# Graph attention on one core: the context is divided on VectorE between two transposes, ScalarE copies two squares of groups 3 to 7, and SyncE's loads and stores stand between two groups' transfers

## The reference, cut to what matters

```
q = _heads(x @ Wq + bq); k = _heads(x @ Wk + bk); v = _heads(x @ Wv + bv)
scores = einsum('bhqd,bhkd->bhqk', q, k) / sqrt(64)
probs  = softmax(scores + where(adj, 0.0, -9e15)[:, None], axis=-1)
ctx    = einsum('bhqk,bhkd->bhqd', probs, v)          # heads put side by side again
out    = layernorm(x + ctx @ Wf + bf)
```

## Time and profile before

| | |
|---|---|
| Median of 3 runs | 1295.83 us (1287.64 to 1299.62) |
| The profiled execution's own time | 1290.07 us |
| Its span on the core | 1288.3 us, granted clock 0.974 |
| Busy share PE / DVE / ACT / POOL | 92% / 76% / 63% / 44% |
| Shares of the chain that ended last | PE 55%, SP's queue 17%, DVE 12%, DMA 7%, ACT 4% |
| DMA engines busy, mean | 76.7% for SyncE's queue, 1.9% for ScalarE's |
| Squares moved by DMA | 1528 from SyncE and 8 from ScalarE, 128 KB each, median 2.4 us from issue to landing |

### The profile page before, as it was taken

The page is one execution under the profiler, slowest core; times in us unless marked ns, Lnnn a source line. Parts: engine busy times, 40 slices in busy tenths (PEclk is TensorE's granted clock), DMA queues, the critical chain, the costliest instruction groups (busy, mean ns, idle before and its releaser), DMA issues.

```text
span 1288.3 us, 24781 instructions
## 1 busy us (share of the span) xinstructions
PE 1187.8 (92%) x8790; PEld 891.4 (69%) x8790; DVE 984.5 (76%) x1535; ACT 807.7 (63%) x1628; POOL 560.8 (44%) x943
## 2 busy tenths in 40 slices
PE   6998999899998899988999989998999889999874
PEld 5866777566776677766787667776777667786653
DVE  5788877778677886878868878688876778778782
ACT  5666765657665676666666676666775657656551
POOL 1234643446524454344543544344643436433432
PEclk9999999999998999989999999999999989999998
DMA  5688787977879777888778888789787887878784
GB/s 161 154 202 228 181 206 189 230 195 176 204 189 237 180 185 196 194 214 203 188 195 194 220 203 210 180 207 239 182 201 199 207 204 174 212 172 203 193 201 109
DMA packets 111611, 251.71 MB, mean 195 GB/s; under 512 B 27904, under 2 KB 62336, under 8 KB 111488
## 3 DMA queue, kind: packets, MB, share of 16 engines
q1 hardware_dynamic: 107296, 243.58, 76.7%
q10 hardware_dynamic: 4192, 6.56, 1.9%
HBM read 36.11 MB, written 12.58 MB: 38 GB/s over the span
## 4 chain that ended last, share of the span: by engine, by line
PE 55%; SPq 17%; DVE 12%; DMA 7%; ACT 4%; issue 4%; POOL 1%; ACTq 0%; POOLq 0%; DVEq 0%
PE context_ps L538 19%; SPq L308 16%; PE score_ps L523 13%; PE job_ps L425 7%; DMA prob_t<-prob 6%; PE job_ps L427 6%; PE job_ps L426 6%; DVE prob L735 6%; DVE prob L728 4%; ACT prob L628 3%; PE job_ps L459 2%; DVE res L750 1%; SPq L388 1%; PE job_ps L435 0%; PE score_ps L435 0%
## 5 line engine op out<-in xcount | busy, mean ns | idle before, releaser
L728 DVE CUSTOM_DVE_ANT_0 prob<-score_ps,mask 128x1024 f32<-128x1024 f32 x384 | 454.8, 1222 | 225.1 <-PE score_ps L523 163.5
L628 ACT ACTIVATE prob<-prob,row_min 128x1024 f32<-128x1024 f32 x384 | 440.2, 1148 | 213.3 <-DVE row_min L728 212.5
L735 DVE STREAM_TRANSPOSE prob<-prob 128x1024 f32<-128x1024 f32 x384 | 457.8, 1230 | 38.8 <-ACT prob L628 38.8
L538 PE MATMUL context_ps<-prob_t,v_all 128*64 128x256 f32 x3072 | 373.0, 398 | 61.9 <-DMA prob_t<-prob 61.8
L538 PEld LDWEIGHTS context_ps<-prob_t,v_all 128*64 128x64 f32 x3072 | 239.4, 144 | 166.9 <-issue 82.1
L850 POOL TENSOR_TENSOR context<-context_raw,context 128x256 f32<-128x256 f32 x96 | 70.8, 738 | 337.5 <-ACT context_raw L645 337.1
L523 PE MATMUL score_ps<-k_hi,q_hi 64*128 64x512 f32 x768 | 141.1, 445 | 4.5 <-DVE row_min L728 3.6
L425 PE MATMUL job_ps<-xt_hi,weight_hi 128*128 128x256 f32 (+1 forms) x423 | 142.0, 336 | 0.0
L427 PE MATMUL job_ps<-xt_hi,weight_lo 128*128 128x256 f32 (+1 forms) x423 | 135.6, 320 | 0.0
L426 PE MATMUL job_ps<-xt_lo,weight_hi 128*128 128x256 f32 (+1 forms) x423 | 135.5, 320 | 0.0
L523 PE MATMUL score_ps<-k_lo,q_hi 64*128 64x512 f32 x768 | 120.9, 392 | 0.0
(11 more groups left out here) (78 smaller groups left out, 1659.5 us busy)
## 6 DMA issues: line engine op xcount, KB each, us to landing
prob_t<-prob SPq DMA_DIRECT2D x1528, 128.0 KB, 2.4
res<-in_x_dram SPq DMA_DIRECT2D x32, 384.0 KB, 4.3
out_dram<-res SPq DMA_DIRECT2D x32, 384.0 KB, 2.9
adj_in<-in_adj_dram SPq DMA_DIRECT2D x31, 256.0 KB, 3.0
x_in<-in_x_dram SPq DMA_DIRECT2D x16, 384.0 KB, 3.5
x_in<-in_x_dram ACTq DMA_DIRECT2D x14, 384.0 KB, 4.5
prob_t<-prob ACTq DMA_DIRECT2D x8, 128.0 KB, 4.8
res<-in_x_dram SPq DMA_DIRECT2D x1, 768.0 KB, 6.8
```

What stands on the lines that cost most here:

```text
L538: last = pe.matmul(context_ps[64 * head:64 * head + 64, 0:GQ], v_all[:, kt, col:col + HS], keys, start=(kt == 0), stop=(kt == TT - 1))
L628: nc.scalar.activation(probabilities(t), probabilities(t), ACT.Exp, scale=-1.0, bias=row_min[:, ring:ring + 1], accum_out=row_sum[:, s // ...
L728: nc.vector.tensor_tensor_reduce(probabilities(t), in_quarters(score_ps[:, head, :]), in_quarters(mask[:, s % 2, :]), 1.0, HUGE, ALU.add, ...
L735: nc.vector.transpose(probabilities(t), probabilities(t)).then_inc(squared, 1)
```

## The change

It has three parts.

1. VectorE multiplies the context straight out of PSUM, between the two turns of the slot that has the mix (`divide` moves from the block of GpSimd to that of VectorE). `take_context`, the buffer `context_raw` and the semaphore `context_out` go; the next mix waits for `context_done` instead.
2. For groups 3 to 7, two of the four squares that stay on their partitions (a = 2 and 3) are no longer moved by DMA: ScalarE copies them (`keep_square`) at the end of slots 2g+2 and 2g+3, one in each, so in slots 8 to 17.
3. SyncE's loads and stores move from odd slots, where they stood between the halves of a group's transfers, to even slots, and the load of the second half of x goes from ScalarE's queue to SyncE's, at slots 12 and 14. Two of GpSimd's additions of the output bias to the residual (`RESIDUALS`) move later with their loads.

```diff
+OWN_GROUPS = (3, 4, 5, 6, 7)
+OWN = (2, 3)
-STORES = {1: -2, 9: -1, 13: 0, 21: 1}
-RES_LOADS = {2: 0, 10: 1, 14: 2, 22: 3}
-X_LOADS = {4: (0, 0), 6: (0, 1)}
-RESIDUALS = {2: -1, 6: 0, 13: 1, 17: 2}
+STORES = {2: -2, 10: -1, 16: 0, 20: 1}
+RES_LOADS = {4: 0, 12: 1, 18: 2, 22: 3}
+X_LOADS = {4: (0, 0), 6: (0, 1), 12: (1, 0), 14: (1, 1)}
+RESIDUALS = {2: -1, 6: 0, 14: 1, 20: 2}
...
                 for a in range(4):
-                    move_square(queue, group, a, (a + ahead) % 4)
+                    if ahead or group not in OWN_GROUPS or a not in OWN:
+                        move_square(queue, group, a, (a + ahead) % 4)
...
             def mix(b, group):
-                pe.wait_ge(context_out, at(b, GROUPS, group + 2))
+                pe.wait_ge(context_done, at(b, GROUPS, group + 2))
...
-            def take_context(b, group):
-                act.wait_ge(mixed, at(b, GROUPS, group + 3))
-                act.wait_ge(context_done, at(b, GROUPS, group + 2))
-                nc.scalar.activation(context_raw[:], context_ps[:, 0:GQ], ACT.Copy).then_inc(context_out, 1)
+            def keep_square(b, group, a):
+                act.wait_ge(squared, at(b, UNITS, 4 * group + 4))
+                act.wait_ge(mixed, at(b, GROUPS, group + 1))
+                own = slice(32 * a, 32 * a + 32)
+                nc.scalar.activation(prob_t[own, group % 2, a].rearrange("p q h n -> p (q h n)"),
+                                     prob[own, group % 2, a].rearrange("p q h n -> p (q h n)"),
+                                     ACT.Copy).then_inc(landed[group % 2], 16)
...
-                        if job[0] == "m":
-                            take_context(b, job[1])
-                        elif job[0] != "p" and job not in early:
+                        if job[0] not in "pm" and job not in early:
                             evict(b, job)
-                            if job == ("x", FT - 1, 0, 1):
-                                for i in range(2):
-                                    load_x(nc.scalar, b, 1, i)
                     for group in contexts_split(b.mode, s):
                         if s - 1 not in SPLIT_LATER:
                             context_high(b, group)
+                    if s // 2 - 1 in OWN_GROUPS:
+                        keep_square(b, s // 2 - 1, OWN[s % 2])
...
+            def divide(b, group):
+                dve.wait_ge(mixed, at(b, GROUPS, group + 3))
+                dve.wait_ge(job_out, out_through(b, ("i", group, 0, 0)))
+                nc.vector.tensor_tensor(context[:], context_ps[:, 0:GQ], context[:],
+                                        ALU.mult).then_inc(context_done, 1)
...
                         turn_squares(b, 2 * s)
+                    for job in work:
+                        if job[0] == "m":
+                            divide(b, job[1])
+                    if s < SLOTS:
                         turn_squares(b, 2 * s + 1)
```

More of the change, by code:

```diff
@@ L157, in graph_attention @@
         raw = sb("raw", [P, 2, 512], F32)
-        context_raw = sb("context_raw", [P, GQ], F32)
         context = sb("context", [P, GQ], F32)
@@ L207, in graph_attention @@
         mixed = sem("mixed")
-        context_out = sem("context_out")
         context_done = sem("context_done")
@@ L419, in _ @@
             pe.sem_inc(mixed, 2)
-            pe.sem_inc(context_out, 2)
             pe.sem_inc(projected, 4)
@@ L702, in _ @@
             dve.sem_inc(masked, 2)
+            dve.sem_inc(context_done, 2)
             dve.sem_inc(sum_done, 8)
@@ L818, in _ @@
             pool.sem_inc(context_lo_done, 1)
-            pool.sem_inc(context_done, 2)
             pool.sem_inc(normalised, 4)
@@ L845, in low_part @@
                 nc.gpsimd.tensor_tensor(lo, copy[:, 0:width], hi, ALU.subtract).then_inc(lo_done, 1)
-            def divide(b, group):
-                pool.wait_ge(context_out, at(b, GROUPS, group + 3))
-                pool.wait_ge(job_out, out_through(b, ("i", group, 0, 0)))
-                nc.gpsimd.tensor_tensor(context[:], context_raw[:], context[:], ALU.mult).then_inc(context_done, 1)
             def context_low(b, group):
@@ L862, in body @@
                     for job in work:
-                        if job[0] == "m":
-                            divide(b, job[1])
                         if job[0] in "kqx":
```

## The result

The changed kernel takes 1247.82 us (median of 4 runs, 1245.41 to 1248.31) against 1297.72 us beside it (1287.64 to 1301.90); the ratio is 0.9623 with a 95% interval of 0.9564 to 0.9681, so it is 3.8% faster. The forecast was 1250, in a range of 1236 to 1272. The profiled execution took 1245.41 us with a span of 1243.6, against a predicted 1249. The runs of the kernel before lie 14.3 us apart, those of the changed kernel 2.9.

The account below looks back on a forecast made before the run. Late squares, from SyncE's issue and x loads, bound slots 8 to 17. Windows fall from 455.47 to 413.6 us (gain 42), tail 2, less 3 for the clock: 41 off 1290.07 gives 1249, predicted 1250, range 1236 to 1272.

Parts of the forecast that it names:

- What bounded the kernel: Slots 8 to 17: TensorE waits 61.8 us for late squares, and a stall also costs about 2 us of slower matmuls.
- The sum of the windows: Slot 8's first mask to slot 17's, eight batches: 413.6 us against 455.47, a gain of 42; one window 51.7.
- Transfers no longer end the waits: Groups 3 to 7: 14 transfers land 11 to 12 us after the last turn; waits on them fall under 10 us.
- three signs of being wrong: Wrong if windows stay above 55 us, mixes still last over 5 us, or copies pass 1.3 us.
- The copy: End of odd slots: ScalarE's copy takes 1.05 us (0.9 to 1.2) and sets the next mask after slots 9, 11, 13.
- The division: VectorE, between the turns: 0.43 us (0.38 to 0.55); even slots take 5.42 to 5.5 us, 0.1 to 0.2 over undisturbed.
- The worth of the division: Gains where ScalarE's high part delayed an exponential, 0.6 us in slot 11, and 2 us in the last batch's tail.
- The share of the order: Slot 12's stall is late issue plus 3.4 us of x, slot 16's issue alone; x now moves while no mix waits.
- The clock: Rival, chance 0.12: slot 14's stall, or summed stalls of slots 10 to 16, bring 1.2 GHz; 1261, up to 1270.
- The slow copy: Rival, chance 0.04: each us of copy over 1.05 costs nearly 4 us a batch; at 2.8 us a copy 1303.
- The tail: Last batch: two short chains behind its mixes go, 0.8 us each, a gain of 2 us.
- The step from the profiled execution to the median: Runs' median lies 5.8 us above the profiled execution, but that spread goes with the stalls: 1249 profiled, 1250 predicted.

Follow-up runs that it names:

- copies_even: The changed kernel with both ScalarE copies of a group at the end of even slot 2g+2, none in odd slots; 1237.90 us, ratio 0.9542.
- the longer copy: The changed kernel with ScalarE first copying 384 more elements in odd slots into a buffer that nothing reads; 1265.89 us.
- one_each: The changed kernel with a group's two copies in even slots, one on ScalarE and one on GpSimd, 14 transfers; 1231.61 us, ratio 0.9501.

## Why the prediction was right, step by step

- **What bounded the kernel.** Right: the late squares of groups 3 to 7 and the slow mixes behind them. The sum of the windows, on which the forecast rests, carries all but 0.2 of the 44.7 us of span.
- **Transfers no longer end the waits.** Right in slots 10 to 18, where ScalarE's copy ended 30 of VectorE's waits. A group of 3 to 7 has landed 11.2 to 11.5 us after its last turn, as said (11 to 12). Waits for transfers were said to fall under 10 us; they are 13.3 and 11.3: TensorE's have one of 6.9 before the last mix, VectorE's are for groups that still have 16 transfers. And of the three signs of being wrong one is there by its words, a mix of over 5 us; it is the last of the kernel and outside the windows that the forecast was about.
- **The copy.** 1054 ns against 1.05 predicted. Slots 9, 11 and 13 take 6.57, 6.56 and 6.33 us against 6.35, 6.35 and 6.1. Two small things were missed: the copy starts 0.03 us after its predecessor's end, not 0.1 before it, and mask and mix start 0.14 after its end, not 0.05. Slot 15 takes 5.60 as predicted, though the sum given for it (5.43 and 0.3) makes 5.73.
- **The division.** 423 ns against 0.43. Even slots take 5.3 us, not 5.42 to 5.5: the predicted lag of 0.1 to 0.2 us lies within the time until the next scores are ready. This error (0.8 us a window) and the copy's (0.7) have opposite signs, so the sum of a window came out at 51.57 against 51.7 by luck as well as by working.
- **The worth of the division.** Here the text was too modest. It named 0.6 us in slot 11 and 2 us at the tail. Alone it is worth nothing that can be seen and on the new order 3 us, under what can be told from nothing, but 22 beside both other parts: without it the square's copy waits behind GpSimd's multiplication, and six mixes fall to the lower clock. I had costed the division against the old ScalarE, not against one with two more copies a group.
- **The share of the order.** The slot 12 stall was put down to 3.4 us of x and a late issue, that of slot 16 to issue alone. The first is borne out: the order alone took 34 us away, 29 of the 30 us by which its windows are shorter lie in slots 11 and 12, and group 4's last square, which had landed up to 3.8 us later than undisturbed, no longer does. What the late issue costs beside x, and what the small loads and stores cost, no run shows by itself. The Trainium skill's sentence that queues share the same engines (Trainium Kernel Development and Optimization, Key Constraints) is not contradicted, but by that rule alone the third part would have cost a little. The landing times show where the gain comes from: the same bytes of x move behind the awaited squares and not in front of them.
- **The clock.** The rival had a chance of 0.12 and did not happen; the 3 us counted for slow mixes in slot 14 were not spent. The border that was read from two rows, 1.92 us on the good side and 2.01 on the bad, is none: in the kernel before itself a mix took 3.67 us after a wait of 3.14, and in copies_even one took 5.36 after 1.79. That 1.66 us did no harm in eight batches is what was forecast, but how safe it is no run shows. By the Trainium skill (TensorE: Matmul & The Clock Gate, Part 1) activity releases the throttle, so a kernel that idles less keeps 2.4 GHz, and the trace after agrees: 1.00 in all eight windows.
- **The slow copy.** It did not happen, but its price was right: nearly 4 us a batch per us. With 0.41 us more on ScalarE's line the longer copy moved four slots by 0.41 us each.

The tail gained 1.1 us instead of 2. The stretches between the windows gained 1.1, and the first window's later start took 1.9 back; neither was in the sum. The step from the profiled execution to the median held too: the spread of the runs went with the stalls, as said. The better version, one_each, shows what the changed kernel left: its copies at the end of odd slots had become the bound (copies_even has them in even slots and takes 10 us less than the changed kernel), and the engine with the most idle time, GpSimd with 40% busy, had no part in them.

## What to carry to other kernels

When a burst of transfers bounds a loop, first look which other loads, from whatever queue, land in front of the square that someone waits for, and put them behind it. Here that was worth 34 us alone, more than taking away an eighth of the burst (25 us), at no engine's cost; once the burst was shorter it was worth 3 us, too little to tell from nothing. Work that an engine takes over belongs where its queue has a gap, not at the slot's end in front of a waiter; price it against the loaded engine as it will be, for a chain that was hidden before (GpSimd's multiplication) may end up in front of it. And parts are not additive: the copies gave 25 us alone, cost 7 on top of the order with the old division, and gave 12 with the new one.

## What had not been expected of the hardware

- A stall of TensorE is not read from one wait. Two waits of 2.31 and 0.41 us with 0.66 us of small matmuls between them left the mix behind them at 5.36 us, in six of eight batches, where the last wait alone would have said nothing. And waits of the same length, 2.05 to 2.07 us, left a mix at 3.67 us in four batches and at 5.36 in four.
- Two loads of 384 KB from ScalarE's queue, issued 1.2 us before the last square of a group from SyncE's, made that square land 5.7 us after its issue and not 2.4.
- GpSimd copied a square of 32 partitions by 1024 float32 in 1029 ns, ScalarE in 1054. But a VectorE instruction on 128x2 elements beside GpSimd's copy took 1.04 us instead of 0.16; in the changed kernel, where ScalarE copies, all 32 of these took 0.16 to 0.17, and the one that ran beside a copy of ScalarE 0.17.
